# Sharing two tiles' loads between two DMA queues in a streaming per-sample matmul

## The reference

```python
def reference(x, itok_B_0_7, L0_cond_weights):
    def mix(x, subjects, weights):
        w = weights[subjects]
        return jnp.einsum('bct,bcd->bdt', x, w)
    return x + mix(x, itok_B_0_7, L0_cond_weights)
```

## Time and profile before

| | us |
|---|---|
| median of three executions | 327.03 |
| the profiled execution, device time | 326.79 |
| its span, from the first instruction to the last | 324.8 |
| TensorE busy | 239.8 |
| VectorE busy | 160.2 |
| ScalarE busy | 130.0 |
| GpSimd busy | 52.7 |
| DMA, mean over the span | 415 GB/s |

### The profile page before, as it was taken

How to read it: one execution, slowest core, us unless ns; L and a number is a source line. 1 busy time by engine, 2 the same in 40 slices (tenths; PEclk the granted TensorE clock), 3 DMA queues, 4 the chain that set the end, 5 groups by cost and what they waited for, 6 DMA issues and landing times.

```text
span 324.8 us, 4203 instructions
## 1 busy us (share of the span) xinstructions
PE 239.8 (74%) x1032; PEld 111.6 (34%) x1032; DVE 160.2 (49%) x130; ACT 130.0 (40%) x129; POOL 52.7 (16%) x137
## 2 busy tenths in 40 slices
PE   3499999999787787786776867768768677687600
PEld 1145555554243343342332332323323333333200
DVE  0437767767546446355354464453544645535410
ACT  1026646556434334334244243342443433424400
POOL 2132122222111111111111011111110111100000
PEclk9979999999999999999999999999999999999955
DMA  7999999999999999999999999999999999999992
GB/s 267 423 422 423 425 427 427 426 426 428 427 428 428 427 427 428 427 428 425 430 424 430 424 428 427 428 427 427 427 428 426 429 426 427 428 426 428 427 428 123
DMA packets 19478, 134.78 MB, mean 415 GB/s; under 512 B 2066, under 2 KB 3091, under 8 KB 3091
## 3 DMA queue, kind: packets, MB, share of 16 engines
q1 hardware_dynamic: 10256, 67.64, 49.7%
q10 hardware_dynamic: 9218, 67.11, 49.0%
HBM read 67.63 MB, written 67.11 MB: 415 GB/s over the span
## 4 chain that ended last, share of the span: by engine, by line
PE 73%; DVE 11%; ACT 5%; issue 2%; DMA 1%; DVEq 1%; POOL 1%; POOLq 1%; ACTq 0%
PE products L140 72%; DVE out_ring L168 10%; ACT out_ring L189 5%; DMA loaded<-weights 1%; DVE table L153 1%; PE products L123 1%; DVEq L37 1%; POOL selected L112 1%; POOLq L107 0%; POOLq L112 0%; ACTq L187 0%; POOLq L101 0%; DVEq L173 0%; POOLq L111 0%; DVEq L152 0%
## 5 line engine op out<-in xcount | busy, mean ns | idle before, releaser
L140 PE MATMUL products<-x_ring,selected 64*128 64x512 f32 x1024 | 234.2, 601 | 61.9 <-DVE out_ring L168 35.0
L168 DVE COPY out_ring<-products 64x1024 f32<-64x1024 f32 x128 | 156.4, 1222 | 140.2 <-PE products L140 138.2
L189 ACT COPY out_ring<-products 64x1024 f32<-64x1024 f32 x128 | 128.7, 1006 | 177.6 <-PE products L140 176.1
L140 PEld LDWEIGHTS products<-x_ring,selected 64*128 64x128 f32 x1024 | 109.3, 188 | 186.7 <-issue 139.3
L112 POOL COPY selected<-table 64x256 f32 x128 | 51.0, 398 | 234.8 <-PE products L140 177.9
L123 PE MATMUL products<-loaded,spread 128*128 128x512 f32 x8 | 5.7, 876 | 5.4 <-DMA loaded<-weights 5.4
L153 DVE TENSOR_TENSOR table<-products,unit 128x1024 f32<-128x1024 f32 x2 | 3.8, 1942 | 9.2 <-PE products L123 9.2
L123 PEld LDWEIGHTS products<-loaded,spread 128*128 128x128 f32 x8 | 2.2, 295 | 8.0 <-issue 8.0
L189 ACT ACT_TABLE_LOAD x1 | 1.3, 1283 | 1.5 <-PEq L210 1.5
L96 POOL TENSOR_SCALAR_AFFINE_SELECT unit<-ones 64x256 f32<-64x256 f32 x2 | 0.8, 404 | 0.1
L88 POOL TENSOR_SCALAR_AFFINE_SELECT spread<-ones 128x256 f32<-128x256 f32 x1 | 0.4, 419 | 0.1
## 6 DMA issues: line engine op xcount, KB each, us to landing
x_ring<-x SPq DMA_DIRECT2D x64, 1024.0 KB, 35.0
out<-out_ring ACTq DMA_DIRECT2D x64, 1024.0 KB, 35.5
loaded<-weights SPq DMA_DIRECT2D x1, 512.0 KB, 4.3
subject_row<-subjects ACTq DMA_DIRECT2D x1, 0.5 KB
```

What stands on the lines that cost most here:

```text
L140: last = nc.tensor.matmul(products[:, b, g, n * BANK:(n + 1) * BANK], selected[part, k, e * mixed:(e + 1) * mixed], x_ring[part, s, e * ti ...
L168: nc.vector.tensor_copy(out_ring[0:HALF, s, b * times:(b + 1) * times], products[b * HALF:(b + 1) * HALF, s % PSUM_BUFS, 0, :]).then_inc(e ...
L189: nc.scalar.copy(out_ring[HALF:channels, s, b * times:(b + 1) * times], products[b * HALF:(b + 1) * HALF, s % PSUM_BUFS, 1, :]).then_inc(o ...
```

## The change

GpSimd loads partitions 0 to 119 of tiles 28 and 29, in a DMA of its own for each, and SyncE only the 8 partitions left. Both are issued at the point at which SyncE issued the whole load: after the product of tile 20, and of tile 21. GpSimd waits for these loads, by semaphores of their own (`x_shared`), before it selects the weights of tile 28; TensorE, which waits for the selection, so waits for them too. SyncE's round of that turn (tiles 24 to 31 are loaded in it) is written out beside the loops, and GpSimd's loop now runs over batches of four tiles: 6 batches, one written out with the DMAs ahead of it, then 9 more. The subject numbers no longer come by ScalarE's queue. GpSimd issues the first 64 as its first instruction, and the other 64 between the two shared loads.

```diff
--- before.py
+++ after.py
@@ -13,6 +13,9 @@
 BANK = 512
 DMA = 16
 HALF = 64
+
+POOL_TILES = (28, 29)
+POOL_ROWS = 120
 
 DRAINED_FREE = 2 * PSUM_BUFS
 PRODUCT_FREE = SELECT_BUFS
@@ -59,6 +62,8 @@
         table_ready = sem("table_ready")
         weights_selected = sem("weights_selected")
         x_loaded = [sem(f"x_loaded{s}") for s in range(TILES_PER_TURN)]
+        x_shared = [sem(f"x_shared{t}") for t in POOL_TILES]
+        rest_loaded = sem("rest_loaded")
         stored = [sem(f"stored{s}") for s in range(TILES_PER_TURN)]
         product_ready = sem("product_ready")
         even_drained = sem("even_drained")
@@ -72,16 +77,27 @@
             for s in range(TILES_PER_TURN):
                 sp.dma_start(x_ring[:, s], x_rows[s * channels:(s + 1) * channels, :]).then_inc(x_loaded[s], DMA)
 
-            with sp.Fori(0, turns - 1) as turn:
+            def go_round(turn, shared=False):
                 for s in range(TILES_PER_TURN):
                     tile = turn * TILES_PER_TURN + s
 
                     sp.wait_ge(product_ready, PRODUCT_FREE + tile + 1)
-                    sp.dma_start(x_ring[:, s], x_rows[bass.ds((tile + TILES_PER_TURN) * channels, channels), :]
+                    a = POOL_ROWS if shared and tile + TILES_PER_TURN in POOL_TILES else 0
+                    sp.dma_start(x_ring[a:, s], x_rows[bass.ds((tile + TILES_PER_TURN) * channels + a, channels - a), :]
                                  ).then_inc(x_loaded[s], DMA)
+
+            before = POOL_TILES[0] // TILES_PER_TURN - 1
+            with sp.Fori(0, before) as turn:
+                go_round(turn)
+            go_round(before, shared=True)
+            with sp.Fori(before + 1, turns - 1) as turn:
+                go_round(turn)
 
         @block.gpsimd
         def _(pool):
+            half = samples // 2
+            pool.dma_start(subject_row[:, :half], subjects.rearrange("(a b) -> a b", a=1)[:, :half]
+                           ).then_inc(subjects_loaded, DMA)
             nc.gpsimd.memset(ones[:], 1.0).then_inc(ones_ready, 1)
             pool.wait_ge(ones_ready, 1)
 
@@ -98,10 +114,9 @@
             pool.wait_ge(subjects_loaded, DMA)
             pool.wait_ge(table_ready, 2)
 
-            with pool.Fori(0, turns) as turn:
-                for s in range(TILES_PER_TURN):
-                    k = s % SELECT_BUFS
-                    tile = turn * TILES_PER_TURN + s
+            def select(batch):
+                for k in range(SELECT_BUFS):
+                    tile = batch * SELECT_BUFS + k
                     for g in range(2):
                         part = slice(g * HALF, (g + 1) * HALF)
                         subject = pool.value_load(subject_row[0:1, bass.ds(2 * tile + g, 1)],
@@ -111,6 +126,25 @@
                             pool.wait_ge(product_ready, PRODUCT_FREE + tile - SELECT_BUFS + 1)
                         nc.gpsimd.tensor_copy(selected[part, k:k + 1, :],
                                               table[part, bass.ds(subject, 1), :]).then_inc(weights_selected, 1)
+
+            shared = POOL_TILES[0] // SELECT_BUFS
+            with pool.Fori(0, shared - 1) as batch:
+                select(batch)
+            for i, tile in enumerate(POOL_TILES):
+
+                pool.wait_ge(product_ready, PRODUCT_FREE + tile - TILES_PER_TURN + 1)
+                pool.dma_start(x_ring[:POOL_ROWS, tile % TILES_PER_TURN],
+                               x_rows[tile * channels:tile * channels + POOL_ROWS, :]).then_inc(x_shared[i], DMA)
+                if i == 0:
+                    pool.dma_start(subject_row[:, half:], subjects.rearrange("(a b) -> a b", a=1)[:, half:]
+                                   ).then_inc(rest_loaded, DMA)
+            select(shared - 1)
+
+            for i in range(len(POOL_TILES)):
+                pool.wait_ge(x_shared[i], DMA)
+            pool.wait_ge(rest_loaded, DMA)
+            with pool.Fori(shared, tiles // SELECT_BUFS) as batch:
+                select(batch)
 
         @block.tensor
         def _(pe):
@@ -175,7 +209,6 @@
 
         @block.scalar
         def _(act):
-            act.dma_start(subject_row[:], subjects.rearrange("(a b) -> a b", a=1)).then_inc(subjects_loaded, DMA)
             act.sem_inc(odd_drained, DRAINED_FREE)
 
             def go_round(turn, first=False):
```

## The result

The changed kernel took 332.80 us (median of four executions, 331.66 to 333.87) against 327.00. The ratio is 1.018, with a 95% interval of 1.015 to 1.021: slower by 1.8%, where I had forecast 0.9% faster. The profiled execution took 332.99 us, with a span of 331.0 against 324.8.

A forecast was written before the change was run, and what follows sets the result against it. Transfers at 427 GB/s were taken to set the pace, with one late DMA engine alone at the end. From 326.79 us, 2.8 of relief and all other terms at nothing gave 324.0; the range was 322.8 to 327.6.

The forecast's parts named there:

- The 120 rows: Loads of tiles 28 and 29: 8 rows to each of 15 engines spare the late one; gain 2.75 to 3.35 us.
- the first rival: Loads of tiles 28 and 29: the relief goes to the wrong engine, 326.8 to 327.4 us, no change; chance 0.20.
- the 2.8 us of relief: End of the kernel: gain from sparing the late engine, the smaller of two ends, 2.75 us, rounded to 2.8.
- SyncE's eight rows: The 8 rows per tile left to SyncE: engines that take two of them end 0.61 us later.
- More code: SyncE's written-out round and GpSimd's loop in three pieces: taken as nothing, 0.3 us kept for the range.
- GpSimd in the middle: GpSimd's issues of tiles 28 and 29 before tile 24's selection: cost nothing from 0.33 to 9 us each.
- The new wait: GpSimd's wait before tile 28's selection: tile 28 may start some 5 us late, but hidden, costing nothing.
- The start: GpSimd's first issue, ahead of its first memset: costs nothing up to 6 us of issue, one for one beyond.
- the third rival: Start: GpSimd's first issue exceeds 6 us; at 10 us, 328.0 or 330.8 us; chance 0.08 shared with the fourth.
- The third queue: GpSimd's queue in mid-kernel: pushes tiles 22 to 27 back by at most 2.45 us and costs nothing.
- The second rival: Loads of tiles 28 and 29: each leaves out another engine, 324.3 or 325.0 us; chance 0.12.
- The fourth: GpSimd's queue deals 15 rows to each of 8 engines: time stays or goes to 331; chance 0.08 shared with third.

The follow-up runs named there:

- shared_only: Changed kernel with the subject numbers whole from ScalarE's queue as before; GpSimd still loads 120 rows of tiles 28 and 29: 332.37 us, ratio 1.0191.
- the extra loads: Changed kernel's code layout, kernel before's work plus four loads of 8 x 4 rows into spare memory: 331.95 us to partitions 4 apart, 337.98 to neighbouring ones.
- code_only: Every DMA, wait and queue of the kernel before, with the changed kernel's code layout: 328.09 us, ratio 1.0042.
- pool_all128: Changed kernel with GpSimd loading all 128 rows of tiles 28 and 29, SyncE none, subject numbers from ScalarE's queue: 327.64 us, ratio 1.0037.
- subjects_only: Changed kernel without the shared loads: subject numbers in two halves from GpSimd's queue, SyncE loads tiles 28 and 29 whole: 327.43 us, ratio 1.0036.
- the probes: Kernel before's work in the changed code layout, plus 16 extra loads of n rows: 327.66 us (n=1), 327.38 (4), 330.89 (5), 333.25 (6), 332.64 (7), 333.52 (8).

## Why the prediction was wrong

**The 120 rows.** This is the step that failed, and twice. I wrote that "what bounds it from the other side is that nothing is gained", and so priced the unknown deal between a gain of 3.35 us and nothing. No row excluded a loss: the trace before has only 128-row deals and one of a single row. The loss was 3.9 us in the changed kernel's windows (3.35 and 0.5), and 1.9% against the kernel before in `shared_only`. Where the loss comes from, the partitions that such rows go to, is shown for the extra loads and likely for these. Second, the relief went to an engine that was not late. That was the first rival, with a chance of 0.20, and it was right in its mechanism, with one engine ahead and ten-odd rows alone at the end, and wrong in its price (326.8 to 327.4), since it took over the same missing loss. I had let the nearness of two numbers, 16 rows of relief and 4.75 us of lateness, stand for evidence about which engine it is; it was evidence about the size only.

Term by term: the 2.8 us of relief became 0. On top came 3.9 for the 120 rows and 1.4 for the code or the start, both of which the sum had at nothing, and the 0.6 for SyncE's rows, which the sum had taken off the relief. The medians say the same: 4.5 us of 327 are 1.4%, and with the 0.4% of the layout that is the 1.8% measured.

**SyncE's eight rows** at 0.61 us: in keeping with the sum of 5.9 out of 6.2, not measured apart.

**More code.** I took nothing and kept 0.3. `code_only` measured 0.42%, 1.4 us, and there is no sign of the mechanism that I named: its page has as many packets of instructions as that of the kernel before, one of 16 KB and three small ones.

**GpSimd in the middle** was right: issues of 0.57, 0.52 and 0.53 us, and the selection of tile 24 at 99.46, far ahead of 107. **The new wait** was right in that it cost nothing: `pool_all128` keeps that wait and stands with `code_only`. GpSimd's loads did not stand behind the work of the other queues: 16.7 us to landing in the changed kernel against 35.0. **The start** was right as far as GpSimd goes. Its first issue took 0.64 us, and `subjects_only` stands with `code_only`; the third rival found no place.

**The third queue** was right too, in `pool_all128`. But my test for it was blind. I wrote that a DMA share under 1 would show the cover broken; it stayed at 1.01 while the rate fell to 362 GB/s.

**The second rival** (each load leaves out another engine) fell: by 319 one engine had stopped for good, some 5 us before the others. Two engines relieved of 8 rows each would have been 8 x 0.307 = 2.5 us ahead, and all 16 at work at 319. The fourth (an uneven deal among few engines) did not occur, since the others stay about level (they stop between 323.4 and 325.2 us); it was the only place at which I let the deal cost anything.

## What to carry to other kernels

A DMA over fewer than 128 partitions is not a shorter 128-partition DMA. Beside other traffic its rows can cost nearly as much again as they take (120 partitions), or little (two halves of 64), and it depends on the partitions that they go to. Before moving work off a late engine, find out which engine it is, with extra rows on the first n engines of the deal, and compare the price of the new deal with the lateness. Read the rate beside the busy share, since a slowed transfer is a busy one.

## What the runs showed of the hardware

- The same 128 extra rows by the same eight engines cost 6.0 us more (337.98 against 331.95, one execution each) when they went to neighbouring partitions in place of partitions 4 apart, in runs of four. Single rows to neighbouring partitions ran at 426 GB/s.
- Loads of 120 partitions lowered the rate of all queues from 427 to 362 GB/s while the DMA engines' busy share stayed at 1.01; the same queue with 128 partitions ran at 426.
- GpSimd's queue takes its turn beside the others: 16.7 us from issue to landing for 960 KB where SyncE's loads took 32.7 in the same execution.
- One DMA engine of 16 is about 4.8 us late at the end, in the kernel before (4.75) and in the changed one (alone from 325.2 to 330.0). By the probes it is one of the fifth to eighth of SyncE's deal, and if it is the same on every chip, the fifth.
- A slow stretch between 24 and 33 us, of 0.6 to 2.1 us by its rate, appears in 11 of 19 profiles of one code layout.
